# A decoder layer on one core: mask order, a piece's place, seven-step roots and unread products in the first group

## Time and profile before

| | us |
|---|---|
| median of 3 runs | 553.97 (553.66 to 554.12) |
| profiled execution, its own time | 554.25 |
| span of the profile | 552.4 |
| PE busy | 525.9 |
| DVE busy | 381.4 |
| ACT busy | 150.3 |
| POOL busy | 128.4 |
| mean granted clock of PE | 0.989 |

### The profile page before, as it was taken

One profiled execution on the slowest core, in us unless ns is written; L12 is line 12 of the kernel. 1 busy time (PEld: TensorE's weight loads), 2 busy tenths in 40 slices (PEclk: granted clock), 3 DMA queues, 4 the chain that ended last, 5 costly groups with the idle time before them and its releaser, 6 DMA issues. The chain is left out here.

```text
span 552.4 us, 8783 instructions
## 1 busy us (share of the span) xinstructions
PE 525.9 (95%) x3303; PEld 430.5 (78%) x3303; DVE 381.4 (69%) x795; ACT 150.3 (27%) x268; POOL 128.4 (23%) x197
## 2 busy tenths in 40 slices
PE   5979999999899999999999999999999999999994
PEld 5736677867788888767888888767888888788884
DVE  3596899888789976875565666875565677833335
ACT  3342101342423222232322112142322111223321
POOL 2020394000016342120014443120014451200001
PEclk9996999999999999999999999999999999999999
DMA  6411431311113110032002110022002110000001
GB/s 190 138 57 43 128 98 58 101 52 40 39 44 120 40 39 11 1 94 98 2 4 64 38 40 11 0 74 80 2 1 66 40 47 2 9 31 1 1 0 39
DMA packets 25274, 26.82 MB, mean 49 GB/s; under 512 B 2832, under 2 KB 22800, under 8 KB 25232
## 3 DMA queue, kind: packets, MB, share of 16 engines
q1 hardware_dynamic: 14080, 15.60, 9.5%
q10 hardware_dynamic: 10720, 9.08, 5.6%
q0 software_dynamic: 432, 1.57, 0.8%
HBM read 24.15 MB, written 2.10 MB: 48 GB/s over the span
## 5 line engine op out<-in xcount | busy, mean ns | idle before, releaser
L1024 PE MATMUL banks<-x2T_lo,ffn_hi 128*128 128x512 f32 (+1 forms) x258 | 110.3, 427 | 1.4 <-ACT inter L632 1.0
L1026 PE MATMUL banks<-x2T_hi,ffn_hi 128*128 128x512 f32 (+1 forms) x258 | 101.2, 392 | 0.0
L1025 PE MATMUL banks<-x2T_hi,ffn_lo 128*128 128x512 f32 (+1 forms) x258 | 101.2, 392 | 0.0
L970 DVE TENSOR_TENSOR inter<-banks,inter 128x512 f32<-128x512 f32 x63 | 43.5, 690 | 80.7 <-PE banks L1026 80.7
L461 POOL TENSOR_TENSOR qbd<-qT_sb,ctxT_sb 128x256 f32<-128x256 f32 x128 | 79.8, 646 | 83.0 <-PE banks L1171 65.5
L1024 PE MATMUL banks<-ffn_lo,inter_hi 128*128 128x256 f32 x256 | 77.2, 301 | 0.7 <-DVE inter_lo L956 0.7
L645 ACT ACTIVATE inter_hi<-inter 128x512 fp32r<-128x512 f32 x63 | 39.8, 631 | 123.6 <-DVE inter L970 123.6
L1025 PE MATMUL banks<-ffn_hi,inter_lo 128*128 128x256 f32 x256 | 71.4, 279 | 0.0
L1026 PE MATMUL banks<-ffn_hi,inter_hi 128*128 128x256 f32 x256 | 71.0, 277 | 0.0
L956 DVE TENSOR_TENSOR inter_lo<-inter,inter_hi 128x512 fp32r<-128x512 f32 x63 | 51.4, 817 | 27.4 <-ACT inter_hi L645 21.6
L632 ACT ACTIVATE inter<-banks 128x512 f32<-128x512 f32 x64 | 38.0, 594 | 118.7 <-PE banks L1026 118.7
(11 more groups left out here) (131 smaller groups left out, 792.6 us busy)
## 6 DMA issues: line engine op xcount, KB each, us to landing
toep_sb<-in_toep ACTq DMA_DIRECT2D x64, 128.0 KB, 2.1
xT_sb<-in_xT SPq DMA_DIRECT2D x4, 512.0 KB, 6.0
ctxT_sb<-in_ctxT SPq DMA_DIRECT2D x4, 512.0 KB, 4.8
x_sb<-in_x SPq DMA_DIRECT2D x4, 512.0 KB, 5.9
ctx_sb<-in_ctx SPq DMA_DIRECT2D x4, 512.0 KB, 6.8
out<-ctxT_sb POOLq DMA_DIRECT2D x3, 512.0 KB, 3.8
raw_w<-in_gate_p SPq DMA_DIRECT2D x8, 128.0 KB, 2.3
raw_s<-in_gate_s SPq DMA_DIRECT2D x8, 128.0 KB
```

Source lines behind the costliest of these rows:

```text
L970: nc.vector.tensor_tensor(inter[:, n % 2, :], up_ps[:, :], inter[:, n % 2, :], ALU.mult).then_inc(inter_ready, 1)
L1024: nc.tensor.matmul(ps, w_hi, x_lo, start=start, stop=False, skip_group_check=True)
L1025: nc.tensor.matmul(ps, w_lo, x_hi, start=False, stop=False, skip_group_check=True)
L1026: return nc.tensor.matmul(ps, w_hi, x_hi, start=False, stop=stop, skip_group_check=True)
```

## The change

It does six things:

1. The roots take `STEPS` = 7 instead of 10 counted steps, 9 DVE instructions instead of 12: the first guess is one instruction, then one step of higher order (four instructions) and one Newton step (three). The result comes without a factor `HALLEY`, which `wide` puts in.
2. `wide` is two ACT instructions, one for each half of the heads; PE's transposes of a half wait for that half.
3. In `heads_of_q`, slot 0, score 1 stands behind `up` instead of behind `down_before`, for groups 1 to 3. On DVE its mask thereby comes ahead of `split`, on POOL and ACT nothing stands between.
4. `SECOND` now names the part ahead of which a slot's piece stands. It is part 2 in slot 5 (behind `up` / `inner` / `inner_hi` and `wide`, ahead of `split`), and part 0 elsewhere, as before.
5. `outproj` on PE runs over the two input tiles outside and the sequences inside, and its first half waits for each half of `factor` by itself.
6. In group 0, 3 unread products stand ahead of PE's wait in `attend` 0 and 4 ahead of each in `attend` 2, 4 and 6; those ahead of `factor` are 11 instead of 14.

```diff
--- before.py
+++ after.py
@@ -36,7 +36,8 @@
 NIBBLE = (1 << 31) | (7 << 22)
 LN_EPS = 1e-5
 RMS_EPS = 1e-5
-STEPS = 10
+STEPS = 7
+HALLEY = 3.0 / 8.0
 
 
 def count(eng, sem, per_group, g, k):
@@ -235,7 +236,8 @@
         opening = scores[:7] + [("squares", 0), scores[7], ("sums", 0), scores[8], ("squares", 1), ("sums", 1),
                                 ("rms", 0), ("wide", 0), ("factor", 0), ("outproj", 0), ("outproj", 1),
                                 ("norm", 0), ("x1T", 0)] + conv
-        heads_of_q = [after(gate=[scores[2 * n]], half=[scores[2 * n + 1]]) for n in range(4)]
+        heads_of_q = [after(gate=[scores[0]], up=[scores[1]])]
+        heads_of_q += [after(gate=[scores[2 * n]], half=[scores[2 * n + 1]]) for n in range(1, 4)]
         slots = heads_of_q + [
             after(gate=[scores[8], ("squares", 0), ("squares", 1)], half=[("sums", 0)], down=[("sums", 1), ("rms", 0)]),
             after(up=[("wide", 0)]),
@@ -251,7 +253,7 @@
 
             return name in ("wide", "factor", "x1T") or name == "score" and k % 2 == 1
 
-        SECOND = [1] * 15 + [0]
+        SECOND = [(2,) if s == 5 else (0,) for s in range(NT - 1)] + [()]
         START = 1
         FIRST = START + 2 + sum(with_piece(*stage) for stage in opening)
         UNITS_FIRST = FIRST + 1
@@ -275,9 +277,9 @@
                     if name in front:
                         front[name](g, k)
 
-            def slot(prev, g, s, times=0, stages=slots):
-                beside(times)
-                for part, follow in zip((gate, up, *down), stages[s] if g is not None else after()):
+            def slot(prev, g, s, pieces_at=(), stages=slots):
+                for i, (part, follow) in enumerate(zip((gate, up, *down), stages[s] if g is not None else after())):
+                    beside(pieces_at.count(i))
                     part(prev, s)
                     run(g, follow)
 
@@ -583,9 +585,11 @@
 
                 count(act, ms_mm, 2, g, 2)
                 count(act, rms_ready, 1, g, 1)
-                nc.scalar.activation(rms_sb[:].rearrange("p k (n e) -> p (k n) e", e=DK),
-                                     inv_rms[:].unsqueeze(2).broadcast_to([P, NB * H, DK]), ACT.Copy)\
-                    .then_inc(wide_ready, 1)
+                rows = rms_sb[:].rearrange("p k t -> p (k t)").rearrange("p (b m h e) -> p b m h e", b=NB, m=KT, e=DK)
+                inv = inv_rms[:].rearrange("p (b m h) -> p b m h", b=NB, m=KT)
+                for mt in range(KT):
+                    nc.scalar.activation(rows[:, :, mt], inv[:, :, mt].unsqueeze(3).broadcast_to([P, NB, HT, DK]),
+                                         ACT.Copy, scale=HALLEY).then_inc(wide_ready, 1)
 
             def x1T(g, _):
                 for j in range(KT):
@@ -765,26 +769,35 @@
             def rms(g, _):
                 count(dve, ms_mm, 2, g, 2)
                 if g:
-                    count(dve, wide_ready, 1, g, 0)
+                    count(dve, wide_ready, 2, g, 0)
                 nc.vector.tensor_scalar(mean_sq[:], fb[0][:, 0:NB * H], 1.0 / DK, RMS_EPS, ALU.mult, ALU.add)\
                     .then_inc(ms_ready, 1)
 
 
                 count(dve, ms_ready, 1, g, 1)
-                nc.vector.tensor_scalar(newton[:].bitcast(I32), mean_sq[:].bitcast(I32), 1, None,
-                                        ALU.logical_shift_right).then_inc(newton_step, 1)
+                nc.vector.tensor_scalar(inv_rms[:].bitcast(I32), mean_sq[:].bitcast(I32), -0.5, 0x5f3759df,
+                                        ALU.mult, ALU.add).then_inc(newton_step, 1)
+
+
                 count(dve, newton_step, STEPS, g, 1)
-                nc.vector.tensor_scalar(inv_rms[:].bitcast(I32), newton[:].bitcast(I32), -1, 0x5f3759df,
-                                        ALU.mult, ALU.add).then_inc(newton_step, 1)
-                for i in range(3):
-                    count(dve, newton_step, STEPS, g, 3 * i + 2)
-                    nc.vector.tensor_tensor(newton[:], inv_rms[:], inv_rms[:], ALU.mult).then_inc(newton_step, 1)
-                    count(dve, newton_step, STEPS, g, 3 * i + 3)
-                    nc.vector.scalar_tensor_tensor(newton[:], newton[:], -0.5, mean_sq[:], ALU.mult, ALU.mult)\
-                        .then_inc(newton_step, 1)
-                    count(dve, newton_step, STEPS, g, 3 * i + 4)
-                    nc.vector.scalar_tensor_tensor(inv_rms[:], newton[:], 1.5, inv_rms[:], ALU.add, ALU.mult)\
-                        .then_inc(rms_ready if i == 2 else newton_step, 1)
+                nc.vector.tensor_tensor(newton[:], inv_rms[:], inv_rms[:], ALU.mult).then_inc(newton_step, 1)
+                count(dve, newton_step, STEPS, g, 2)
+                nc.vector.tensor_tensor(newton[:], newton[:], mean_sq[:], ALU.mult).then_inc(newton_step, 1)
+                count(dve, newton_step, STEPS, g, 3)
+                nc.vector.scalar_tensor_tensor(newton[:], newton[:], -10.0 / 3.0, newton[:], ALU.add, ALU.mult)\
+                    .then_inc(newton_step, 1)
+                count(dve, newton_step, STEPS, g, 4)
+                nc.vector.scalar_tensor_tensor(inv_rms[:], newton[:], 5.0, inv_rms[:], ALU.add, ALU.mult)\
+                    .then_inc(newton_step, 1)
+
+                count(dve, newton_step, STEPS, g, 5)
+                nc.vector.tensor_tensor(newton[:], inv_rms[:], inv_rms[:], ALU.mult).then_inc(newton_step, 1)
+                count(dve, newton_step, STEPS, g, 6)
+                nc.vector.scalar_tensor_tensor(newton[:], newton[:], -0.5 * HALLEY ** 2, mean_sq[:], ALU.mult, ALU.mult)\
+                    .then_inc(newton_step, 1)
+                count(dve, newton_step, STEPS, g, 7)
+                nc.vector.scalar_tensor_tensor(inv_rms[:], newton[:], 1.5, inv_rms[:], ALU.add, ALU.mult)\
+                    .then_inc(rms_ready, 1)
 
             def factor(g, _):
                 count(dve, oraw_ready, 2, g, 2)
@@ -1062,6 +1075,8 @@
 
                 mt, b = v // 4, v % 4
                 count(pe, v_ready, 2, g, 2)
+                if g == 0 and v % 2 == 0:
+                    keep_clock(3 + (v > 0), down_ps[1])
                 count(pe, sm_ready, 16, g, 2 * v + 2)
                 into = o_half(mt)[:, b // 2, b % 2 * S:(b % 2 + 1) * S] if g else fb[2 + mt][:, b * S:(b + 1) * S]
                 for odd in range(2):
@@ -1123,10 +1138,10 @@
             def factor(g, _):
 
                 if g == 0:
-                    keep_clock(14, down_ps[1])
-                count(pe, wide_ready, 1, g, 1)
+                    keep_clock(11, down_ps[1])
                 wide = rms_sb[:].rearrange("p k t -> p (k t)")
                 for mt in range(KT):
+                    count(pe, wide_ready, 2, g, mt + 1)
                     for b in range(NB):
                         at = b * D + mt * P
                         last = nc.tensor.transpose(fb[mt][:, b * S:(b + 1) * S], wide[:, at:at + P], ident[:])
@@ -1135,12 +1150,13 @@
             def outproj(g, j):
                 if g == 0 and j == 0:
                     keep_clock(2, down_ps[1])
-                count(pe, on_ready, 2, g, 2)
-                for b in (2 * j, 2 * j + 1):
-                    for kt in range(KT):
+                for kt in range(KT):
+                    count(pe, on_ready, 2, g, 2 if j else kt + 1)
+                    for b in (2 * j, 2 * j + 1):
                         last = nc.tensor.matmul(fb[j][:, (b % 2) * D:(b % 2 + 1) * D],
                                                 o_sb[:, kt, b * S:(b + 1) * S], wo_sb[:, kt, :],
-                                                start=kt == 0, stop=kt == KT - 1)
+                                                start=kt == 0 and b % 2 == 0, stop=kt == KT - 1,
+                                                skip_group_check=True)
                 last.then_inc(wo_mm, 1)
 
             def x1T(g, _):
```

## The result

The changed kernel took 545.72 us (median of 4 runs, 544.87 to 546.93) beside 553.82 us for the one before (551.03 to 554.12); the ratio is 0.9882, with a 95% interval of 0.9855 to 0.9909. The forecast was 545.6.

The account below looks back on a forecast made before the run. PE, busy 525.9 of 552.4 us, was taken as the bound, so only its idle or slow time could be won. 554.25 - 4.3 - 2.9 - 1.15 = 545.9, forecast as 545.6 us because the profiled run lay 0.3 above the median; range 544.6 to 549.2.

Parts of the forecast that it names:

- Unread products between the scores: Group 0's opening: 15 more products fill PE's 1.13 us waits at no cost of their own; the clock holds.
- The sums' part of 1.96 us: Group 0's opening: with the clock held, the roots start at 47.2 instead of 49.16, 1.96 us earlier.
- the whole of the opening: Group 0 up to its projection: all parts there together save 4.3 us, bounds 4.0 and 4.6.
- First rival: Group 0's opening: the clock falls all the same near 44.7; opening gives 0.9 instead of 4.3, 549.0 us; chance 0.18.
- Roots: Roots in group 0's opening: nine DVE instructions instead of 12 save 0.78 us.
- `wide` and the order of the projection: Opening: halves of `wide` at 0.6 us each, first transposes about 50.2; the projection's new order worth nothing there.
- Second sequence ahead of the low part: Slot 0, groups 1 to 3: mask 1 ahead of `split` ends PE's wait; saves 2.9 us, bounds 2.6 and 3.2.
- new waits at `attend` 2: Sign of being wrong: PE gets new waits there; the forecast had `attend` 2 come forward by 0.8 us.
- A piece behind inner: Slot 5, group 1's roots: waits for `gelu` and `wide` go; saves 1.15 us, bounds 0.6 and 1.5.

Follow-up runs that it names:

- e5: The kernel before, run again without any edit: 552.11 us.
- e3: The changed kernel with score 1 of slot 0 back behind `down_before`, so its mask again stands behind the low part: 548.51 us.
- e1: The changed kernel without the 15 unread products between the first group's scores: 545.55 us.
- e6: The changed kernel without the 15 unread products between the scores, run once more for more executions: 545.77 us.
- e2: The kernel before with only the 15 unread products between the scores added: 550.88 us, ratio 0.9977.
- e8: The changed kernel with transposes and projection waiting for both halves of `wide` and `factor`, projection in the old loop order: 546.31 us.
- e4: The changed kernel with all pieces at the start of their slots, slot 5 too: 545.71 us.
- e9: The changed kernel with the roots in ten counted steps and all pieces at the start of their slots: 546.97 us.
- e12: The changed kernel with the pieces behind opening scores 1 and 3 and `factor` taken out, extra pieces in slots 12 and 14: 546.21 us.

## Why the prediction was right, and where not

**The number** was right, 545.6 for 545.72. What was wrong is what it was measured against. The prediction took the fall of the clock near 44.7 us as part of the kernel before, and it is part of some of its executions: a third have a low mean clock. The profile was of such a one (clock 0.989), and so, by their times of 553.66 and more, were the three runs shown. In the executions with a mean clock of 0.995 or more before takes 551.0, and against these the change is worth 5.3 us, not the 8.4 that the forecast took off. The traces give the same: from the first mask to the end of the span 520.43 us (e5) and 514.96 (after), 5.5 less, of which 0.86 come in the opening, 1.45 at the roots of group 1 and 3.1 from the order of the masks (e3).

**What was luck.** The number is no proof of the step that carried most of it. The changed kernel without the products took 545.55 us (e1), and a fall came in one of ten such executions; four runs of the changed kernel would likely have shown about 545.7 whatever the products do. The forecast is an absolute time, so it came out right as soon as the clock held, for whichever reason.

**Unread products between the scores** ("I take it that the clock holds"): it held in the traces. The sums' part of 1.96 us measured 1.72, the whole of the opening 4.2 for 4.3. (The 1.96 is not quite what its rows give: 44.8 + 0.64 + 0.60 + 0.95 is 47.0, not 47.2. On that scale the roots started at 47.44, with 1.03 us for the sums instead of 0.95.) But of these, 3.3 come only where the clock would have fallen, and 0.86 otherwise (34.79 to 33.93). The busy shares that I compared (75% of a pair, 67% of the last stretch) don't explain the fall either: executions that held had the same 67%. In e1, PE was busy for 2.28 of the 3.40 us ahead of 44.9 us, and the clock stayed at 1.00; in e6 for 2.27 in the same stretch, and it fell. That the products cost nothing was right: e2 and the held execution of before have the same 23.91.

**First rival**, that the clock falls all the same: no trace with the products shows it. The Trainium skill (TensorE: Matmul & The Clock Gate, Why this matters for your kernels) asks for no long idle gaps between bursts. The measurement goes beyond it: in e6 PE's longest idle time in the 17 us ahead of the fall is 1.13 us, shorter than what the page speaks of, and the clock fell. With fillers in just these gaps the kernel before had no low clock in ten executions, where the rule alone gave them no part in it. The measurement decides, as far as ten executions can.

**Roots**: 0.78 forecast, 0.73 measured in the opening.

**`wide` and the order of the projection**: "worth nothing here" for the opening was near (0.17 us in e8); in slot 6 their share is 0.60 us at the projection.

**Second sequence ahead of the low part**: 2.9 us forecast, 2.8 by the time of e3, and 0.85 for group 1 by the trace (first mask to the mean_sq of group 1: 110.50 in e3, 109.65 after), for 0.8 forecast. I had also seen mask 2 as what is late next, and had named new waits at `attend` 2 as a sign that I am wrong. One came, 0.23 us; the mechanism held all the same. In the prediction, mask 2 follows mask 1 by 3.20 + 0.62 us; it measured 3.81 (110.97 to 114.78). The 0.62 stands there without a row, where `split` had taken 1.14; it was right for the reason given in the last section.

**A piece behind inner**: 1.15 us forecast. The step as a whole measured 1.45 from mean_sq to the convolution of group 1 (24.66 to 23.21). But the forecast let `factor` move by the piece's place alone, and that is the term that failed: undone alone it costs 0.2 us or nothing (e4). The shorter roots already get the piece, `gelu` and `wide` forward; the forecast gave them nothing in this group, since `inner` waits for `up`. The two are covers of each other (e9: 0.86 us at `factor` and 0.95 at the convolution with both undone), and the rest, 0.60 (e8), is the projection that starts on the first half of `factor`, which the forecast had counted in the same term with about 0.5. That forecast should have asked what the place is worth once the roots are shorter.

## What to carry to other kernels

A profile is one execution. Before a stall or a slow clock in it is made a term of a sum, compare the run's mean granted clock with those of other runs: here a third of the executions of one program had a low mean clock and took 1.3 to 4.3 us more than the median of the others, and three runs happened to show nothing else. A forecast that comes out right as an absolute time can still be wrong about what the change is worth. Fillers in short gaps are likely insurance against such a fall, and were free where another engine set the pace. And of two edits on one wait, cost each with the other in place: two that each remove it are worth it once.

## What had not been expected of the hardware

The clock can fall in one execution and hold in the next of the same program: of two traces of the kernel before, with idle times of PE that agree to 0.01 us ahead of 44 us, one has the fall and the other not, and so it is for e6 and e1. Where a fall stands in the opening's chain it came at 44.7 us in one trace and about 45.8 in the other, both while PE ran sums and narrow matmuls. It ended about 10 us later: at 54.9 us in the row of 14 products of 512 columns, and in e6 near 56.0, when that row was over and PE ran the transposes. What decides whether it comes is open.

DVE beside POOL: `split`, with two inputs in SBUF, took 1.14 us beside POOL's spreading of q, and 0.68 after the change, where the mask (one input in PSUM) lies beside POOL instead and keeps its 1.23. POOL's row before and after:

```profile
114.39 0.61 POOL L417 TENSOR_TENSOR qbd<-qT_sb,pair_sel 128x256 f32<-128x256 f32 x1 [12.93 <-PE banks L1091]
...
111.03 0.61 POOL L419 TENSOR_TENSOR qbd<-qT_sb,pair_sel 128x256 f32<-128x256 f32 x1 [12.92 <-PE banks L1106]
```

With the old order back (e3) `split` takes 1.13 us again. So the new order saved 0.46 us of DVE as well. In e12 the low part of a piece took 1.12 us beside POOL's products, where 0.68 is usual, and POOL's 1.99 for two, where 1.21 is. The Trainium skill (GPSIMD Engine Reference, Specifications) says that the two share SBUF interfaces, with contention for DVE instructions with two SBUF inputs; the traces agree, with these numbers.
